# Deltas a tile ahead in layer 0, from stacked bf16 parts in layer 1, and odd Fourier frequencies folded once more

## The reference

```python
h = relu(bn(einsum('bnc,hc->bnh', x, w1)))          # 192 channels, 1024 positions
X = fft(h, axis=1, norm='ortho')
xr = relu(X.real * rd - X.imag * idg + rb)
xi = relu(X.imag * rd + X.real * idg + ib)
y = ifft(xr + 1j * xi, axis=1, norm='ortho').real
return bn(einsum('bnh,ch->bnc', y, w2))
```

## Time and profile before

| | us |
|---|---|
| median of 3 runs | 20652.78 |
| profiled execution | 20652.02 |
| its span, first to last instruction | 20649.6 |
| TensorE busy | 18375.9 (89%) |
| VectorE busy | 17104.8 (83%) |
| ScalarE busy | 15878.6 (77%) |
| GpSimd busy | 13914.1 (67%) |
| granted TensorE clock, share of full | 0.954 |

### The profile page before, as it was taken

The page is one execution under the profiler, slowest core; times in us unless marked ns, Lnnn a source line. Parts: engine busy times, 40 slices in busy tenths (PEclk is TensorE's granted clock), DMA queues, the critical chain, the costliest instruction groups (busy, mean ns, idle before and its releaser), DMA issues. The chain is left out here.

```text
span 20649.6 us, 269196 instructions
## 1 busy us (share of the span) xinstructions
PE 18375.9 (89%) x75272; PEld 10312.5 (50%) x75272; DVE 17104.8 (83%) x12555; ACT 15878.6 (77%) x24714; POOL 13914.1 (67%) x6884
## 2 busy tenths in 40 slices
PE   7699997899967899898899999999999999789798
PEld 2355553455532344334465566656665666245353
DVE  2889998899966599568899999999999999755666
ACT  6499995899943555566799999999999999234545
POOL 0189993799934488345599999999999999000101
PEclk8799997899988999999999999999999999799999
DMA  4578885788874421466633333333333333810303
GB/s 120 189 237 241 241 244 189 227 241 242 245 208 125 169 78 72 167 231 244 260 116 126 117 126 116 127 116 127 117 126 120 124 126 106 211 49 26 91 28 85
DMA packets 842734, 3173.83 MB, mean 154 GB/s; under 512 B 101542, under 2 KB 124682, under 8 KB 816140
## 3 DMA queue, kind: packets, MB, share of 16 engines
q1 hardware_dynamic: 805900, 3030.56, 45.7%
q10 hardware_dynamic: 35328, 125.85, 1.9%
HBM read 2317.15 MB, written 838.88 MB: 153 GB/s over the span
## 5 line engine op out<-in xcount | busy, mean ns | idle before, releaser
L1542 DVE TENSOR_TENSOR_SCAN l1s_h<-l1s_da,l1s_pd 128x1024 f32<-128x1024 f32 x3072 | 6820.7, 2273 | 330.1 <-PE l1s_pd L1477 244.4
L1580 ACT ACTIVATE l1s_dm<-l1s_dut,l1s_bt 128x384 f32<-128x384 f32 x7680 | 4187.8, 604 | 19.9 <-PE l1s_pd L1477 19.3
L1563 ACT ACTIVATE l1s_da<-l1s_dl,l1s_a 128x1024 f32<-128x1024 f32 x3072 | 3498.2, 1139 | 74.6 <-DVE l1s_h L1542 53.6
L1477 PE MATMUL l1s_pd<-l1s_id,l1s_dm 128*128 128x128 f32 x23040 | 3055.7, 274 | 155.5 <-DVE l1s_h L1542 106.8
L1477 PEld LDWEIGHTS l1s_pd<-l1s_id,l1s_dm 128*128 128x128 f32 x23040 | 2629.8, 142 | 821.9 <-issue 534.8
L1446 POOL TENSOR_TENSOR l1s_sm<-l1s_h 128x1024 f32<-128x1024 f32 x1024 | 2435.0, 2378 | 170.4 <-DVE l1s_h L1542 170.4
L1451 POOL TENSOR_TENSOR l1s_pb<-l1s_h,l1s_cc 128x1024 f32<-128x1024 f32 x1024 | 2437.2, 2380 | 1.4 <-DMA l1s_cc<-crows 0.7
L1455 POOL TENSOR_TENSOR l1s_pa<-l1s_sm,l1s_cc 128x1024 f32<-128x1024 f32 x1024 | 2434.4, 2377 | 0.0
L853 POOL TENSOR_TENSOR dw_acc<-dw_acc,dw_prod 128x961 f32<-128x961 f32 (+3 forms) x704 | 1573.6, 2276 | 1003.7 <-ACT dw_prod L806 995.6
L1487 PE MATMUL l1s_py<-l1s_pb,l1s_id 128*128 128x512 f32 x4096 | 2014.5, 614 | 222.8 <-POOL l1s_pb L1451 222.8
L2112 POOL CAST ffn_h<-ffn_z 128x1024 fp8e5<-128x1024 f16 x128 | 181.2, 1416 | 2903.4 <-DVE ffn_z L2132 2898.1
(11 more groups left out here) (302 smaller groups left out, 32193.8 us busy)
## 6 DMA issues: line engine op xcount, KB each, us to landing
l1s_cc<-crows SPq DMA_DIRECT2D x1024, 512.0 KB, 3.7
l0sf_cc<-l0crowsf SPq DMA_DIRECT2D x512, 512.0 KB, 5.6
l0sb_cc<-l0crowsb SPq DMA_DIRECT2D x512, 512.0 KB, 5.5
l0sf_cc<-l0crowsf SPq DMA_DIRECT2D x512, 256.0 KB, 7.3
l0sb_cc<-l0crowsb SPq DMA_DIRECT2D x512, 256.0 KB, 7.1
dls<-l1p_dl SPq DMA_DIRECT2D x192, 512.0 KB, 7.0
duts<-l1p_dut SPq DMA_DIRECT2D x64, 1536.0 KB, 5.8
l1s_dut<-duts SPq DMA_DIRECT2D x64, 1536.0 KB, 7.2
```

The source lines that it names most:

```text
L1477: mm = pe.transpose(pd[:, s % 2, blk * 128:blk * 128 + 128], dm[:, rnd % 2, blk, j * 128:j * 128 + 128], idt[:, :])
L1542: dve.tensor_tensor_scan(h[:, s % 4, :], da[:, j, :], pd[:, s % 2, :], 0.0, ALU.mult, ALU.add)\
L1563: act.activation(da[:, j, :], dl[:, half, j, :], ACT.Exp, scale=a[:, HT * half + j, n:n + 1])\
L1580: ins = act.activation(dm[:, rnd % 2, blk, :], dut[:, half, blk, :], ACT.Identity, scale=bt[:, half, blk, n:n + 1])
```

## The change

Layer 0: `minus_abs` becomes a bitwise OR of the sign bit from `pd` into `ab`; `softplus`, behind the tap group, makes `max(p, 0) + ln` from `pd` and `ln` into `dl` in one instruction. GpSimd has no work left in the stage. `pd` is now held until `softplus`. TensorE computes the deltas of the next tile at the start of each step.

Layer 1: the projection gives `dt` in nine copies of columns and, by a fifth matmul of bf16 ones, rows of ones; ScalarE copies all 128 rows of `px` to bf16 (`hi`) and B and C to `bc`; VectorE subtracts (`rest`), ScalarE copies rows 64 on to bf16 (`mid`), VectorE subtracts again (`lo`), so that `parts` holds high, middle and low parts of `dt`, stacked. The weights are cut into three bf16 parts at the start of the stage. The deltas are then one bf16 matmul for each half. VectorE takes the OR and, a step later, the max-add, in halves; the product with u goes to GpSimd.

Attention: the odd frequencies are 8j+1 and 8j+5 instead of 2j+1; VectorE makes `pq` and `tz` from `td`, so that each set needs two matmuls of 256 columns instead of four of 512 for both; the even transform goes first. The inverse gives two quarters, which VectorE puts together (`ov`, `vd`) and adds with a factor.

```diff
-                            dve.wait_ge(s_dl[p], (k - p) * 8)
-                        dve.wait_ge(dtm, nth(T * k + t))
-                        dve.tensor_scalar(dl[:, p, t, :], pd[:, (s + t) % 2, :], 0.0, None, ALU.max).then_inc(plus, 1)
-                        dve.wait_ge(plus, nth(T * k + t))
-                        dve.wait_ge(expd, nth(T * (k - 1) + t))
-                        dve.scalar_tensor_tensor(out=ab[:, t, :], in0=dl[:, p, t, :], scalar=-2.0, in1=pd[:, (s + t) % 2, :],
-                                                 op0=ALU.mult, op1=ALU.add).then_inc(absd, 1)
+                        if here(k):
+                            dve.wait_ge(dtm, nth(T * k + t))
+                            dve.wait_ge(expd, nth(T * (k - 1) + t))
+                            dve.tensor_scalar(ab[:, t, :].bitcast(I32), pd[:, (s + t) % 2, :].bitcast(I32), SIGN, None, ALU.bitwise_or).then_inc(absd, 1)
+
+                    def softplus(t):
+
+                        if here(k):
+                            if t == 0:
+                                dve.wait_ge(s_dl[p], (k - p) * 8)
+                            dve.wait_ge(lnd, nth(T * k + t))
+                            dve.scalar_tensor_tensor(out=dl[:, p, t, :], in0=pd[:, (s + t) % 2, :], scalar=0.0, in1=ln[:, t, :],
+                                                     op0=ALU.max, op1=ALU.add).then_inc(sumd, 1)
 
                     for t in range(T):
                         times_u(t)
+                        minus_abs(t)
                         convolve(t)
-                        minus_abs(t)
+                        softplus(t)
                     convolve(3)
 
...
+                        pe.wait_ge(sumd, nth(T * k + t - 2))
                         for hs in HALVES:
...
                     for t in range(T):
+                        if t < T - 1:
+                            deltas(k, s, t + 1)
+                        else:
+                            deltas(k + 1, s + 1, 0)
                         turn_du(t)
-                        deltas(t)
                         if t < 2:
...
+                            q = T * k + t
+                            pool.wait_ge(sumd, nth(2 * q + 1))
+                            pool.wait_ge(dutm, nth(q - 2))
+                            pool.tensor_tensor(du[:, t % 2, :], dl[:, t, :], in_order(s, t), ALU.mult).then_inc(dud, 1)
...
+                            dve.wait_ge(expd, nth(q - 3))
+                            for i, hs in enumerate(HALVES):
+                                dve.wait_ge(dtm, nth(2 * q + i))
+                                dve.tensor_scalar(ab[:, t % 3, hs].bitcast(I32), pd[:, t % 2, hs].bitcast(I32), SIGN, None,
+                                                  ALU.bitwise_or).then_inc(absd, 1)
+                        m, v = back(k, t, 1)
+                        if there(m):
...
-                            dve.wait_ge(dtm, nth(q))
-                            dve.tensor_scalar(dl[:, t, :], pd[:, t % 2, :], 0.0, None, ALU.max).then_inc(plus, 1)
-                            dve.wait_ge(plus, nth(q))
-                            dve.wait_ge(expd, nth(q - 3))
-                            dve.scalar_tensor_tensor(out=ab[:, t % 3, :], in0=dl[:, t, :], scalar=-2.0,
-                                                     in1=pd[:, t % 2, :], op0=ALU.mult, op1=ALU.add).then_inc(absd, 1)
-                        m, v = back(k, t, DU)
-                        if there(m):
-                            dve.wait_ge(sumd, nth(T * m + v))
-                            dve.wait_ge(dutm, nth(T * m + v - 2))
-                            dve.tensor_tensor(du[:, v % 2, :], dl[:, v, :], in_order(s + (t - DU) // T, v), ALU.mult)\
...
+                            dve.wait_ge(lnd, nth(q))
+                            for hs in HALVES:
+                                dve.scalar_tensor_tensor(out=dl[:, v, hs], in0=pd[:, v % 2, hs], scalar=0.0,
+                                                         in1=ln[:, v % 3, hs], op0=ALU.max, op1=ALU.add).then_inc(sumd, 1)
+                        if t == 2 and there(k + 1):
+                            dve.wait_ge(hi, nth(k + 1))
+                            dve.wait_ge(mid, nth(k))
+                            dve.tensor_tensor(rest[GROUPS, :], px[GROUPS, :], parts[GROUPS, p, :], ALU.subtract).then_inc(res, 1)
+                        if t == 3 and there(k + 1):
+                            dve.wait_ge(mid, nth(k + 1))
+                            dve.tensor_tensor(parts[96:128, p, :], rest[96:128, :], parts[96:128, p, :], ALU.subtract)\
+                               .then_inc(lo, 1)
 
...
-                                mm = pe.matmul(px[:, hs], wsum[:, c, :], row[:, hs], start=(c == 0), stop=(c == 3))
+                                pe.matmul(px[:, hs], wsum[:, c, :], row[:, hs], start=(c == 0), stop=False)
+                            mm = pe.matmul(px[:, hs], one_at[:, :], one_row[:, hs], start=False, stop=True)
...
-                        pe.wait_ge(dtc, nth(m))
-                        pe.wait_ge(absd, nth(T * m + v - 2))
-                        for hs in HALVES:
-                            mm = pe.matmul(pd[:, v % 2, hs], wd[:, v, :], dts[:, (s + (t + 2) // T) % 2, hs],
+                        pe.wait_ge(lo, nth(m))
+                        for i, hs in enumerate(HALVES):
+                            pe.wait_ge(sumd, nth(2 * (T * m + v - 2) + i))
+                            mm = pe.matmul(pd[:, v % 2, hs], wdel[:, v, :], parts[:, (s + (t + 2) // T) % 2, hs],
                                            start=True, stop=True)
-                        mm.then_inc(dtm, 1)
+                            mm.then_inc(dtm, 1)
...
+                        pe.wait_ge(bcd, nth(k + 1))
+                        pe.wait_ge(res, nth(k + 1))
...
-
-                    def read():
-                        act.wait_ge(xd, nth(k + 1))
-                        act.wait_ge(dtm, nth(T * (k - 1) + T - 1))
-                        act.wait_ge(btm, nth(k - 1))
-                        act.wait_ge(s_c[p], (k + 1 - p) * 8)
-                        act.activation(dts[0:XD, p, :], px[0:XD, :], ACT.Copy).then_inc(dtc, 1)
-
                     for t in range(T):
                         m, v = back(k, t, OUT)
                         if there(m):
...
+                            act.activation(*place(s, v), ACT.Copy).then_inc(dutc, 1)
+                        if t == 2 and there(k + 1):
+                            act.wait_ge(xd, nth(k + 1))
+                            act.wait_ge(dtm, nth(2 * (T * (k - 1) + T - 1) + 1))
+                            act.activation(parts[:, p, :], px[:, :], ACT.Copy).then_inc(hi, 1)
+                            act.wait_ge(btm, nth(k - 1))
+                            act.wait_ge(s_c[p], (k + 1 - p) * 8)
+                            act.activation(bc[0:2 * N, p, :], px[0:2 * N, :], ACT.Copy).then_inc(bcd, 1)
                         if there(k):
                             q = T * k + t
-                            act.wait_ge(absd, nth(q))
-                            act.wait_ge(sumd, nth(q - 3))
+                            act.wait_ge(absd, nth(2 * q + 1))
+                            act.wait_ge(sumd, nth(2 * (q - 3) + 1))
                             act.activation(ln[:, t % 3, :], ab[:, t % 3, :], ACT.Exp).then_inc(expd, 1)
                             act.wait_ge(expd, nth(q))
                             act.activation(ln[:, t % 3, :], ln[:, t % 3, :], ACT.Ln, bias=1.0).then_inc(lnd, 1)
                         if t == 2 and there(k + 1):
-                            read()
+                            act.wait_ge(res, nth(k + 1))
+                            act.activation(parts[GROUPS, p, :], rest[GROUPS, :], ACT.Copy).then_inc(mid, 1)
                         if t == 4 and there(k + 1):
                             act.wait_ge(btm, nth(k + 1))
                             act.wait_ge(s_bt[p], (k + 1 - p) * 8)
...
-                            bank = px[:, c, 2:4].rearrange("p g a f -> p (g a f)")
-                            for t in range(TT):
...
-                                mm = pe.matmul(bank, td[:, p, t, chunk], fo[:, t, :], start=(t == 0), stop=(t == TT - 1))
-                            mm.then_inc(dft, 1)
...
                                 for t in range(TT // 2):
                                     mm = pe.matmul(px[:, c, e].rearrange("p a f -> p (a f)"), te[:, p, e, t, chunk],
                                                    fe[:, e, t, :], start=(t == 0), stop=(t == TT // 2 - 1))
+                            mm.then_inc(dft, 1)
+                        for c in range(2):
+                            chunk = slice(c * H2, (c + 1) * H2)
+                            for g in range(2):
+                                if c == 0:
+                                    pe.wait_ge(spin, nth(4 * k + 2 + g))
+                                for a in range(2):
```

(34 more changed lines are left out.)

152 lines of the change are left out of this document (86 added, 66 removed).

## The result

The changed kernel takes 20912.87 us (median of 4 runs, 20907.92 to 20924.05) against 20649.74 (4 runs, 20644.06 to 20653.59) of the kernel before beside it: 1.0127 times, 95% interval 1.0112 to 1.0142. The predicted time was 20874, the range 20580 to 20960. The profiled execution took 20908.61 us, its span is 20906.8 against 20649.6, +257.2.

What follows compares the result with a forecast made beforehand. VectorE was taken to bound layer 0's scan inputs, TensorE layer 1's, and a ring between engines attention. The terms -178 + 251 + 5 + 144 = +222 gave 20874 us, range 20580 to 20960.

Steps and rivals of the forecast that it cites:

- Layer 0, -178: Layer 0's two scan-input stages: stretched VectorE instructions and a wait go, short stalls come; 89 us gained a stage.
- in 14 full turns: Layer 0's scan inputs: each full turn gains 6.0 us, 84 us a stage.
- about 5 more in the last two turns: Layer 0's scan inputs: about 5 us further gain in the last two turns, which waited for TensorE at every tile.
- Layer 1's scan inputs, +251 and +5: A turn of 35.1 us against 26.9, +8.1 x 31; about 5 us once for cutting the weights into parts.
- two such places: Layer 1's turn: half clock costs 2.1 us at B's transposes with the tile's behind them, 2.1 at the projection.
- Attention, +144: Attention of layers 2 and 3: ring +0.3 us, half clock after TensorE's pause +2.1, so +2.4 x 60 turns.
- The other 16.8 ms have the same instructions before and after: Stages outside the changed ones: same instructions, no time difference in the sum.
- (1): Rival: the clock stays up because the pauses are shorter than 6.7 us; 20618 us, chance 0.15.
- (2): Rival: the clock falls in one of the two kinds of stage, or every other turn; 20700 to 20800, chance 0.15.
- (3): Rival: in layer 1 the projection is ready in time, ScalarE's own bound of 22 us a turn; 20473, chance 0.08.
- (4): Rival: layer 1's low part stretched by 2.2 us, or layer 0's new wait longer; 20950, chance 0.10 with (5).
- (5): Rival: layer 0's deltas wait for the previous tile's max-add, none really ahead; +90 on the forecast, chance 0.10 with (4).

Runs made afterwards that it cites:

- l1_ahead: Changed kernel with layer 1's projection put ahead of the deltas of tile 3 on TensorE; 20837.88 us.
- l1_behind: Changed kernel with ScalarE's two copies of the projection put behind the exponential and logarithm of tile 2 again; 20874.59 us.
- l1_split: Changed kernel with layer 1's projection cut into four pieces, one ahead of the deltas in each of four steps, its copies moved later; 20563.45 us.
- best_old: Changed kernel with the attention of before and layer 1's projection in four pieces, everything of it one step earlier than in l1_split; 20361.00 us.
- l1_warm: Changed kernel with 12 more f32 matmuls on TensorE behind the projection's copies in each turn of layer 1's scan inputs; 20843.81 us.

## Why the prediction was right, point by point

- **Time and sign.** Right, 39 us under the measured time. But the closeness is in part luck, owed to errors that cancel: 35 us of gain expected in layer 0 that did not come, 52 us too much loss in layer 1's scan inputs, 45 us in a stage that the sum left at nothing, and 4 to 5 in attention.
- **Layer 0, -178, measured -143** (-158 as a part alone). The mechanism was right term by term in the steady turn: stretches gone, the OR from PSUM at 1.22 us, stalls 2.85, 0.29, 0.52 for 2.7, 0.3, 0.45, turn 27.06 for 26.9. The mis-sized terms are "in 14 full turns" and "about 5 more in the last two turns". From one product with u to the same of the next turn (L394, now L387) there are thirteen full turns in the forward stage, not fourteen, and five of them take 27.6 to 28.6 us: together 356.7 us instead of 429.4, 72.7 less for the 84. The last two turns, forecast 5 us shorter, are 2.2 longer: VectorE waits for ScalarE there, 13.9 and 16.2 us.
- **Layer 1's scan inputs, +251 and +5, measured +204.** The chain was right from link to link: ScalarE idling 8.2 us for the projection (7 to 10 was the mark set), the exponential of tile 2 behind the copies, and l1_ahead and l1_behind each shortened it by undoing one link, l1_split by undoing several. Without the loss of clock the turn was to be 30.9 and is 31.7. The term too large is the clock's, "two such places", 2.1 + 2.1: B's transposes and the tile's behind them ran at half, but the projection ran at full in 25 of 29 turns, although TensorE had only the short deltas and transposes to do ahead of it. An inner turn grew by 6.7 us for the 8.1 of the sum. Marked by ScalarE's exponentials (L1327, now L1363), the 31 turns take 211 us more, for 251; the start of the stage takes 0.4 more, for 5; and its end behind the last turn 7.5 less, which the sum did not have.
- **Attention, +144, measured +148.** Pause 5.7 us predicted, 5.70 measured; output sums 4.66 and 4.69; wait for the sums of all tiles 2.9 (2.26 + 0.56 + 0.1) and 2.87. The clock cost 2.7 us a steady turn for 2.1 taken, and the steady turn grew by 3.1 for 2.4. That the stage came out right is luck: the kernel before also had longer turns of 29.2 us, and the first two turns, 29.2 and 30.7 us before, are 25.3 and 28.4 now.
- **The step that failed** is none in the sum but one ahead of it: "The other 16.8 ms have the same instructions before and after" was taken to mean the same time. It cost 45 us, through the clock (24 stretches of half clock for 8), a cost that the sum priced in the changed stages alone.
- **Rivals.** (1), the clock stays up, fell: 0.87 and 0.78. (2), half of it, is nearest to what layer 1 did, with one place of two, but its time, 20700 to 20800, was not met. (3), ScalarE's own bound, did not occur in the changed kernel, but its turn was priced right for another order: 22 us, where best_old's is 22.1. (4)'s stretched low part did not occur: L1276 never met GpSimd's product and took 1.22 us each time. In best_old it meets it in 30 of 32 turns and takes up to 2.24 us, with 1.15 us of overlap:

```profile
L1276 DVE TENSOR_TENSOR l1p_parts<-l1p_rest,l1p_parts x32: 1222/1346/2239, 9237.6 to 9919.1; 32x1024 bf16<-32x1024 f32 x32
```

  (5) did not occur: in the changed kernel VectorE waits for layer 0's deltas (L395) once in the forward stage, 3.2 us.

## What to carry to other kernels

Before taking work from an engine, ask what of its work stands on the ring and what it does in the time that comes free: two of the three parts of this change took work from TensorE and got slower, since what came free turned into pauses, half clock and a new link between engines. When an engine's order is fixed by program, a long operation (here 7.3 us of projection) belongs in pieces between the short ones, and whatever reads it behind the work that is ready; the two together, which were not tried apart, were worth 349 us here, more than the 263 that the change cost. And compare stages, not totals: one run gave the expected total for another reason.

## What the hardware did that was not expected

- An unchanged stage of 7.3 ms ran 45 us (0.6%) longer for what came before it: 24 stretches of half clock against 8 (23 to 29 in the runs with most half clock ahead of the stage), and back to 8 after 300 us of dense matmuls ahead of it.
- The granted clock fell without a long pause: after 3.3 us with TensorE busy 1.35, with no idle piece longer than 1.74 us (l1_warm).
- A stand of TensorE of 5.7 us cost 2.7 us a turn in attention, and 4.5 us of matmuls whose result nobody reads gave it back.
- VectorE's bitwise OR from PSUM on int32 views takes 1.22 us for 1024 elements (L395) and 0.68 for 512 (L1259), as the max-add out of PSUM does (1.23 at L403, 0.68 at L1268).
